# Splitting the first input tiles in two groups of four, with half a Q slice computed in between

## The chip, the cores and the metric

The kernel runs on one core of a Trainium2 chip. The metric is the device time of one execution in microseconds. The engines are PE (TensorE, matrix products), DVE (VectorE), ACT (ScalarE), POOL (GpSimd) and SP (SyncE, which here only issues transfers). They run side by side and wait for one another by semaphores.

## The reference

The input x has 4 batches of 1024 tokens with 1024 features. Two layers are computed:

```
x = x + attention(layernorm(x), Wq, bq, Wk, bk, Wv, bv)     # 16 heads of 64
x = x + layernorm(x) @ (ffn_weight * scale[:, None]).T + ffn_bias
layernorm(x) = (x - mean(x)) / sqrt(var(x) + 1e-5)          # no gain, no bias
```

The attention is local: a block of 128 queries sees 256 keys, 64 of them on either side of the block. 64 tokens of each head (the first, the last, and the 62 with the largest norm of q) see all 1024 keys instead. All is float32; the kernel gets that precision from PE by splitting each operand in a high and a low part (x = hi + lo) and summing three products, hi\*hi, hi\*lo and lo\*hi.

## The kernel before, in words

**Tiles.** A batch is 8 input tiles of 128 tokens by 1024 features (TILES = 8). The normalised batch stands transposed and split in xT_hi and xT_lo. The weights come in 24 slices of 128 output columns for each batch: 8 of Q, then 8 pairs of V and K. A slice is projected in two halves of 512 tokens (PSUM banks proj[0] and proj[1]). A half is 24 products of 128x128 by 128x512: 8 of w_hi with xT_hi, 8 of w_lo with xT_hi, 8 of w_hi with xT_lo (`project`, L439). `project_half` can issue them in two parts of 12.

**The order of the work** is written out by hand, one program for each engine. Every engine has an outer loop over the 4 batches (on PE at L628), and inside it loops over pairs of Q slices and over head pairs. In each batch PE projects the Q slices (`project_q`), then alternates attention of a head pair with the projections of the next (`attend`). Beside the last head pair of a batch (`ahead` is False) the tiles of the next batch are turned and split, so that the first projection of the next batch follows at once.

**The beginning of the program** has no attention to hide behind. For its 8 tiles:
- SP (L213 to L221) loads tiles 0 and 1, four small columns of constants (semaphore const_in, 64 when all are in), tiles 2 and 3, and each of tiles 4 to 7 when the tile four before it has landed; then two weight slices (L225) and the bias row.
- POOL (`split`, L324 and L326) makes w_hi and w_lo of weight slices 0 and 1 when they have landed.
- DVE waits for const_in, takes the moments of the tiles (`moments`, L895: two bn_stats a tile), and computes 1/sqrt of all 8 variances in one chain (`roots`, L908 to L918: 14 links, each waiting for the one before). Then it normalises each tile in place (`normalise`, L928) and subtracts for the low half (`rows_lo`, L960, two operations a tile), two tiles behind.
- PE turns each normalised tile by 8 transposes (`turn_rows`, L462), alternately into the banks of proj and of turn. Tile t waits for the low half of tile t - 2, which frees its bank.
- ACT casts the turned tile into xT_hi (`rows_hi`, L691, two operations a tile). The first activation of the program is preceded by the load of ACT's table.

When all 8 low halves are there (semaphores xT_set, waited for at the head of PE's outer loop), PE starts with slice 0.

Of the kernel before, what the change touches and what calls it, by code (L numbers as in the profile page):

```python
# [53 lines left out]
def build(nc, rows_in, wstream, bq, bk, bv, scale_ffn, bias_ffn, out):  # L54
# [7 lines left out]
    with ExitStack() as ctx:  # L62
# [134 lines left out]
        LAST_TILES = [[0], [1], [2], [3], [4], [5], [6], [7]]  # L197
        proj_banks, turn_banks = [proj[:, h, :] for h in range(2)], [turn[:, h * 512:h * 512 + 512] for h in range(2)]
# [231 lines left out]
        def _(pe):  # L430
# [195 lines left out]
            for t in range(TILES):  # L626
                turn_rows(q_store[:, t, :], t, (proj_banks, turn_banks)[t % 2], 2)
            with pe.Fori(0, BATCH) as n:  # L628
                for h in range(2):
                    pe.wait_ge(xT_set[h], (n + 1) * TILES)  # L630
                apart(pe)
                project_half(n, 0, 0, n * BUFS, 0)
                with pe.Fori(0, PAIRS // 4) as j:
                    project_q(n, j)
                project_q(n, PAIRS // 4, norms_too=True)
                with pe.Fori(PAIRS // 4 + 1, PAIRS // 2) as j:
                    project_q(n, j)
                project_half(n, PAIRS, 0, n * BUFS + PAIRS // 2, 1, (0,))
                turn_norms(n, 1)
                project_half(n, PAIRS, 0, n * BUFS + PAIRS // 2, 1, (1,))  # L640
                for half in range(2):
                    project_half(n, PAIRS + 1, 1, n * BUFS + PAIRS // 2, half)
                with pe.Fori(0, PAIRS - 1) as hp:
                    attend(n, hp, True)
                attend(n, PAIRS - 1, False)

# [34 lines left out]
        def _(act):  # L681
            for h in range(2):
                act.sem_inc(proj_free[h], 1)
            act.wait_ge(const_in, 64)
# [147 lines left out]
            for t in range(TILES):  # L832
                rows_hi(t, t, (proj_banks, turn_banks)[t % 2])
# [36 lines left out]
        def _(dve):  # L870
# [9 lines left out]
            dve.wait_ge(const_in, 64)  # L880
# [4 lines left out]
            def link_of(steps, links):  # L885
# [13 lines left out]
            def roots(steps, size=1, weight_scale=None):  # L899

                links = [1]
                link = link_of(steps, links)
                var, minus_half, bits, rstd, sq, less = (x[:, 0:size] for x in (ln_var, ln_minus_half, ln_bits, ln_rstd,
                                                                                ln_sq, ln_less))
                dve.wait_ge(ln_step, steps + 1)
                apart(dve)
                for i in range(size):
                    last = dve.bn_aggr(ln_mv[:, i, :], ln_stats[:, i, :, :].rearrange("p a b -> p (a b)"))  # L908
                link(last)
                dve.tensor_scalar(minus_half, ln_mv[:, 0:size, 1], EPS, -0.5, ALU.add, ALU.mult)  # L910
                link(dve.tensor_scalar(var, ln_mv[:, 0:size, 1], EPS, None, ALU.add))
# [19 lines left out]
            FIRST_STEPS = LN_LINKS  # L931
# [237 lines left out]
            for t in range(TILES):  # L1169
                dve.wait_ge(first_in[t % 4], 16 * (t // 4) + 16)  # L1170
                moments(q_store[:, t, :], t, last=(t == TILES - 1))
            roots(0, TILES)
            for t in range(TILES):
                normalise(q_store[:, t, :], q_store[:, t, :], t, xn_set)
                if t >= 2:
                    rows_lo(t - 2, t - 2, (proj_banks, turn_banks)[t % 2])
            for t in range(TILES - 2, TILES):
                rows_lo(t, t, (proj_banks, turn_banks)[t % 2])
# [104 lines left out]
```

## Time and profile before

| | |
|---|---|
| median of 3 runs | 2288.05 us (2286.37 to 2288.64) |
| the profiled execution | 2291.68 us, its span 2290.1 us |
| PE busy | 2194.3 us, 96% |
| DVE, ACT, POOL busy | 67%, 36%, 26% |
| granted clock of PE, mean | 0.989 of full speed |

The page's 40 slices cover 57 us each. Only in the first is PE poorly used (4 tenths). The granted clock reads 9 tenths or more in all slices but one. The chain that ended last runs over PE for 78% of the span and over DVE for 15%.

How to read it: busy time counts an engine as busy while an instruction of its is open. "issue" in the chain of waits is time in which an engine waited for nothing that the profile shows. An instruction can be open, and so count as busy, while it is waiting for something that no semaphore shows.

### The profile page before, as it was taken

The numbers are of one execution on the slowest core, as the hardware profiler recorded it, in microseconds if no ns is written. First come the engines' busy times: TensorE is split into PE (matmuls) and PEld (weight loads), VectorE is DVE, ScalarE is ACT, GpSimd is POOL, SyncE is SP. The second block draws the span as 40 slices with busy tenths as digits, with TensorE's granted clock in tenths as the row PEclk, the third lists the DMA queues.
The fourth block names the chain that finished last, engine by engine and source line by source line (L and its number), as shares of the span: only waits on it lengthen the run. The fifth ranks groups of instructions, "written<-read, shape, count | busy, mean of one in ns | idle before, by whom it ended". The sixth has DMA issues, their size and how long they took to land.

```text
span 2290.1 us, 41027 instructions
## 1 busy us (share of the span) xinstructions
PE 2194.3 (96%) x13024; PEld 1863.8 (81%) x13024; DVE 1536.3 (67%) x3450; ACT 835.2 (36%) x2201; POOL 601.6 (26%) x468
## 2 busy tenths in 40 slices
PE   4999999989999999899999998999999988999999
PEld 3878888868788888787888887878888876888887
DVE  5587776653877765738777657297776676666664
ACT  2224444443254454532444445224544450000000
POOL 1232232223232231232322312324123123222211
PEclk9999999999999999999999999999999998999999
DMA  3321111112211111123111110231111113333331
GB/s 120 87 89 43 51 58 43 49 34 79 89 48 53 58 41 50 32 78 92 49 51 53 46 53 31 65 97 58 39 51 60 40 33 139 126 135 137 137 129 73
DMA packets 106440, 160.04 MB, mean 70 GB/s; under 512 B 9648, under 2 KB 75254, under 8 KB 106352
## 3 DMA queue, kind: packets, MB, share of 16 engines
q1 hardware_dynamic: 98416, 140.03, 18.7%
q10 hardware_dynamic: 4608, 16.78, 1.8%
q0 software_dynamic: 3328, 2.17, 0.5%
q8 instruction: 42, 0.69, 0.1%
q14 instruction: 46, 0.38, 0.1%
HBM read 107.53 MB, written 51.41 MB: 69 GB/s over the span
## 4 chain that ended last, share of the span: by engine, by line
PE 78%; DVE 15%; issue 4%; ACT 2%; DVEq 0%; DMA 0%; SPq 0%; ACTq 0%
PE proj L439 36%; PE proj L661 15%; PE pv L532 8%; PE turn L522 5%; PE score L507 4%; PE pv L577 3%; PE score L558 2%; DVE x_norm L1003 2%; DVE top_idx L1001 2%; DVE top_val L999 2%; PE misc L545 1%; PE turn L652 1%; DVE q_sq L966 1%; DVE norms L968 1%; PE turn L568 1%
## 5 line engine op out<-in xcount | busy, mean ns | idle before, releaser
L439 PE MATMUL proj<-xT_hi,w_hi 128*128 128x512 f32 x1536 | 404.3, 405 | 11.8 <-issue 8.4
L439 PE MATMUL proj<-xT_hi,w_lo 128*128 128x512 f32 x1536 | 406.5, 398 | 0.0
L439 PE MATMUL proj<-xT_lo,w_hi 128*128 128x512 f32 x1536 | 381.0, 390 | 0.0
L439 PEld LDWEIGHTS proj<-xT_lo,w_hi 128*128 128x128 f32 x1536 | 288.3, 188 | 61.7
L439 PEld LDWEIGHTS proj<-xT_hi,w_lo 128*128 128x128 f32 x1536 | 283.9, 189 | 63.2
L439 PEld LDWEIGHTS proj<-xT_hi,w_hi 128*128 128x128 f32 x1536 | 276.9, 190 | 68.7 <-issue 11.3
L757 ACT ACTIVATE probs<-score,neg_max 128x256 f32<-128x256 f32 (+1 forms) x512 | 229.1, 460 | 165.2 <-DVE neg_max L1048 99.4
L334 POOL TENSOR_TENSOR ctx_out<-pv_sum,row_inv 128x256 f32<-128x256 f32 x128 | 87.9, 687 | 705.9 <-DVE pv_sum L1085 705.9
L326 POOL TENSOR_TENSOR w_lo<-w_raw,w_hi 128x1024 fp32r<-128x1024 f32 x98 | 243.4, 2483 | 7.9
L324 POOL CAST w_hi<-w_raw 128x1024 fp32r<-128x1024 f32 x98 | 106.1, 1083 | 501.7 <-PE proj L439 313.0
L532 PE MATMUL pv<-v_nat,pT_lo 128*128 128x128 f32 x1024 | 198.3, 275 | 0.0
L532 PE MATMUL pv<-v_nat,pT_hi 128*128 128x128 f32 x1024 | 194.3, 271 | 3.1 <-DVE pT_lo L1064 2.8
L1085 DVE TENSOR_TENSOR pv_sum<-pv,pv_lo 128x256 f32<-128x256 f32 x128 | 54.2, 424 | 185.5 <-ACT pv_lo L781 185.5
L966 DVE TENSOR_TENSOR q_sq<-q_nat 128x512 f32<-128x512 f32 x64 | 63.1, 986 | 168.4 <-ACT q_nat L707 167.4
L532 PEld LDWEIGHTS pv<-v_nat,pT_hi 128*128 128x128 f32 x1024 | 161.6, 191 | 15.5 <-issue 5.6
L1064 DVE TENSOR_TENSOR pT_lo<-turn,pT_hi 128x512 fp32r<-128x512 f32 x256 | 164.7, 684 | 11.5 <-ACT pT_hi L770 9.1
L532 PEld LDWEIGHTS pv<-v_nat,pT_lo 128*128 128x128 f32 x1024 | 155.4, 192 | 0.0
L419 POOL TENSOR_TENSOR q_store<-q_store,bias_b 128x1024 f32<-128x1024 f32 x32 | 76.6, 2396 | 286.4 <-DVE q_store L1232 284.9
L770 ACT CAST pT_hi<-turn 128x512 fp32r<-128x512 f32 x256 | 138.8, 597 | 7.7 <-PE turn L522 2.0
L522 PE MATMUL turn<-ident,probs 128*128 128x128 f32 (+1 forms) x1024 | 138.2, 277 | 3.5 <-ACT probs L757 3.5
L698 ACT ACTIVATE qT_cur<-proj,bq_c 128x512 f32<-128x512 f32 x64 | 44.1, 689 | 234.0 <-PE proj L439 234.0
L522 PEld LDWEIGHTS turn<-ident,probs 128*128 128x128 f32 (+1 forms) x1024 | 112.8, 138 | 6.6 <-ACT probs L757 6.5
(139 smaller groups left out, 3596.3 us busy)
## 6 DMA issues: line engine op xcount, KB each, us to landing
w_raw<-in_wstream SPq DMA_DIRECT2D x98, 512.0 KB, 3.8
q_store<-in_rows SPq DMA_DIRECT2D x36, 512.0 KB, 3.4
x_buf<-in_rows SPq DMA_DIRECT2D x36, 512.0 KB, 3.3
q_rows<-q_nat SPq DMA_DIRECT2D x64, 256.0 KB, 2.3
ctx_rows<-ctx_out SPq DMA_DIRECT2D x128, 128.0 KB, 1.8
q_store<-ctx_rows SPq DMA_DIRECT2D x32, 512.0 KB, 4.1
out<-q_store ACTq DMA_DIRECT2D x32, 512.0 KB, 2.6
bias_b<-in_bias_ffn SPq DMA_DIRECT2D x1, 512.0 KB, 7.6
```

The lines of the kernel that those rows point to most:

```text
L324: pool.tensor_copy(w_hi[b][:, :], w_raw[b][:, :]).then_inc(w_hi_set, 1)
L326: pool.tensor_tensor(w_lo[b][:, :], w_raw[b][:, :], w_hi[b][:, :].bitcast(F32), ALU.subtract).then_inc(w_split[b], 1)
L334: pool.tensor_tensor(ctx_out[:, s % 2].rearrange("p b h d -> p h b d"), pv_sum[:, s % 2].rearrange("p (h b) d -> p h b d", h=2), row_inv[: ...
L439: mm = pe.matmul(proj[:, half, :], w[b][:, k * P:k * P + P], x[:, k, half * HALF:half * HALF + HALF], start=(m == 0), stop=(m == 23), skip ...
L507: mm = pe.matmul(score[:, at:at + hi - lo], qs[r, i * BLK:i * BLK + BLK], ks[r, lo:hi], start=(first and b == 0), stop=stop, skip_group_ch ...
L522: mm = pe.transpose(turn[0:rows, col:col + P], probs[:, src:src + rows], ident[:, :])
L532: mm = pe.matmul(pv[:, g * P:g * P + P], pt[:, (g * 2 + c) * P:(g * 2 + c) * P + P], v_nat[:, 2 * s + b + c, h, :], start=(m == 0), stop=( ...
L661: mm = pe.matmul(proj[:, half, :], x[b][:, k * P:k * P + P], w[:, k, half * 512:half * 512 + 512], start=(m == 0), stop=(m == 23), skip_gr ...
L757: last = act.activation(probs[:, at:at + hi - lo], score[:, at:at + hi - lo], ACT.Exp, bias=neg_max[:, g:g + 1], accum_out=row_sum[:, g:g ...
L770: act.copy(pT_hi[:, h * 512:h * 512 + 512], turn[:, h * 512:h * 512 + 512]).then_inc(pT_hi_set, 1)
L966: dve.tensor_tensor(q_sq[:, :], src, src, ALU.mult).then_inc(q_squared[h], 1)
L1064: dve.tensor_tensor(pT_lo[:, cols], turn[:, cols], pT_hi[:, cols].bitcast(F32), ALU.subtract).then_inc(pT_set, 1)
```

## The change

Engine by engine:
- **DVE.** It no longer waits for const_in ahead of the first moments (it does so behind the last low half). Three operations on one column (q_sq from zero_c) are added at the top, of the kinds tensor_scalar with add and mult, tensor_scalar with a shift, and tensor_tensor with mult. `roots` can now work on four of the eight columns (`at`) and call a function between two links (`between`). The chain is run twice, for tiles 0 to 3 with the moments of tiles 4 to 6 between its links, and for tiles 4 to 7 with the low halves of tiles 0 to 2 between them.
- **ACT.** Instead of the wait for const_in there is a copy of one column of the identity at the top. The wait for const_in stands ahead of the last tile.
- **PE.** The turned tiles go to the banks of score and turn, so that proj is free. When tiles 0 to 3 are split the first part (12 products) of slice 0, half 0 is issued behind tile 4, the second part behind tile 5. The outer loop runs over 3 batches; each ends with the first half slice of the next, and the last batch stands as a copy behind the loop.

```diff
+        score_banks = [score[:, h * 512:h * 512 + 512] for h in range(2)]
+        FIRST = TILES // 2
...
-            for t in range(TILES):
-                turn_rows(q_store[:, t, :], t, (proj_banks, turn_banks)[t % 2], 2)
-            with pe.Fori(0, BATCH) as n:
+            def first_turn(t):
+                turn_rows(q_store[:, t, :], t, (score_banks, turn_banks)[t % 2], 2)
+
+            def first_q(n, tiles, part):
+                if part == 0:
+                    for h in range(2):
+                        pe.wait_ge(xT_set[h], tiles)
+                    apart(pe)
+                project_half(n, 0, 0, n * BUFS, 0, (part,))
+
+            def batch(n):
                 for h in range(2):
                     pe.wait_ge(xT_set[h], (n + 1) * TILES)
                 apart(pe)
-                project_half(n, 0, 0, n * BUFS, 0)
...
+            for t in range(FIRST):
+                first_turn(t)
+            first_turn(FIRST)
+            first_q(0, FIRST, 0)
+            first_turn(FIRST + 1)
+            first_q(0, FIRST, 1)
+            for t in range(FIRST + 2, TILES):
+                first_turn(t)
+            with pe.Fori(0, BATCH - 1) as n:
+                batch(n)
+                for part in range(2):
+                    first_q(n + 1, (n + 2) * TILES, part)
+            batch(BATCH - 1)
...
-            act.wait_ge(const_in, 64)
+            act.wait_ge(ident_set, 1)
+            act.copy(probs[:, 0:1], ident[:, 0:1])
...
-            dve.wait_ge(const_in, 64)
+            dve.wait_ge(edge_zero, 1)
+            dve.tensor_scalar(q_sq[:, 0:1], zero_c[:, :], EPS, -0.5, ALU.add, ALU.mult)
+            dve.tensor_scalar(q_sq[:, 1:2].bitcast(U32), zero_c[:, :].bitcast(U32), 1, None, ALU.logical_shift_right)
+            dve.tensor_tensor(q_sq[:, 2:3], zero_c[:, :], zero_c[:, :], ALU.mult)
...
             def link(ins):
                     links[0] += 1
                     ins.then_inc(ln_step, 1)
+                    if between is not None:
+                        between(links[0])
                     dve.wait_ge(ln_step, steps + links[0])
...
+            def late_moments(k):
+                if k % 3 == 0 and k < 3 * FIRST:
+                    first_moments(FIRST + k // 3 - 1)
+            def early_lo(k):
+                if k % 3 == 0 and k < 3 * FIRST:
+                    first_lo(k // 3 - 1)
+            for t in range(FIRST):
+                first_moments(t)
+            roots(0, FIRST, between=late_moments)
+            dve.wait_ge(first_in[3], 32)
+            moments(q_store[:, TILES - 1, :], TILES - 1)
+            for t in range(FIRST):
+                first_normalise(t)
+            roots(LN_LINKS, FIRST, at=FIRST, between=early_lo)
+            first_normalise(FIRST)
+            first_lo(FIRST - 1)
+            for t in range(FIRST + 1, TILES):
+                first_normalise(t)
+                first_lo(t - 1)
+            first_lo(TILES - 1)
+            dve.wait_ge(const_in, 64)
```

How this moves the instructions. First PE at the beginning of the program, before (L462 turns a tile, L439 are the products of a projection):

```order
L462 MATMUL turn<-ident,q_store 128x128 x8
L462 MATMUL proj<-ident,q_store 128x128 x8
L462 MATMUL turn<-ident,q_store 128x128 x8
L628 UNCONDITIONAL_BRANCH
L628 ISA
L447 ISA
```

and now, from tile 3 on (L464 turns a tile, L441 is a projection):

```order
L464 MATMUL turn<-ident,q_store 128x128 x8
L464 MATMUL score<-ident,q_store 128x128 x8
L441 MATMUL proj<-xT_hi,w_hi 128x512 x8
L441 MATMUL proj<-xT_hi,w_lo 128x512 x4
L464 MATMUL turn<-ident,q_store 128x128 x8
L441 MATMUL proj<-xT_hi,w_lo 128x512 x4
L441 MATMUL proj<-xT_lo,w_hi 128x512 x8
L464 MATMUL score<-ident,q_store 128x128 x8
L464 MATMUL turn<-ident,q_store 128x128 x8
L664 UNCONDITIONAL_BRANCH
```

The 24 products of slice 0, half 0 stand among the turns of tiles 5 to 7 and no longer behind them.

On DVE, the moments and the first links of the chain, before (L895 are moments, L908 to L916 the chain):

```order
L895 BN_STATS ln_stats<-q_store 128x6 x16
L908 BN_AGGR ln_mv<-ln_stats 128x2 x8
L910 TENSOR_SCALAR ln_minus_half<-ln_mv 128x8
L911 TENSOR_SCALAR ln_var<-ln_mv 128x8
L912 TENSOR_SCALAR ln_bits<-ln_var 128x8
L913 TENSOR_SCALAR ln_rstd<-ln_bits 128x8
L916 TENSOR_TENSOR ln_sq<-ln_rstd 128x8
```

and now (L926 are moments, L939 to L947 the chain, on four columns):

```order
L926 BN_STATS ln_stats<-q_store 128x6 x8
L939 BN_AGGR ln_mv<-ln_stats 128x2 x4
L941 TENSOR_SCALAR ln_minus_half<-ln_mv 128x4
L942 TENSOR_SCALAR ln_var<-ln_mv 128x4
L926 BN_STATS ln_stats<-q_store 128x6 x2
L943 TENSOR_SCALAR ln_bits<-ln_var 128x4
L944 TENSOR_SCALAR ln_rstd<-ln_bits 128x4
L947 TENSOR_TENSOR ln_sq<-ln_rstd 128x4
L926 BN_STATS ln_stats<-q_store 128x6 x2
```

The moments of tiles 4 to 6 come between the links of the first chain.

On PE at the end of a batch, before (L577 is the last product of the attention, L628 the outer loop, L652 the second layer, behind it):

```order
L462 MATMUL proj<-ident,q_store 128x128 x8
L577 MATMUL pv<-v_nat,pT_hi 128x256 x9
L577 MATMUL pv<-v_nat,pT_lo 128x256 x9
L628 REGISTER_ALU
L628 COMPARE_AND_BRANCH
L652 MATMUL turn<-ident,x_norm 128x128 x8
```

and now (L579 is the last product of the attention, L664 the outer loop, L642 the first inner loop of the next batch or of the copy):

```order
L579 MATMUL pv<-v_nat,pT_lo 128x256 x9
L634 ISA
L449 ISA
L450 ISA
L441 MATMUL proj<-xT_hi,w_hi 128x512 x8
L441 MATMUL proj<-xT_hi,w_lo 128x512 x8
L441 MATMUL proj<-xT_lo,w_hi 128x512 x8
L664 REGISTER_ALU
L664 COMPARE_AND_BRANCH
L642 UNCONDITIONAL_BRANCH
```

Before, the branch of the outer loop (L628) stood directly behind the last product of pv, and the half slice was the first thing behind its target.

## Rows read from the trace of the kernel before

**Rows 1.** Chain of waits, 0 to 60 us: start us, us, what.
```profile
6.79 9.60 DVE ln_stats L895 x16
...
24.65 0.82 DVE q_store L928
...
26.89 1.28 ACT L691
...
30.09 0.72 DVE q_store L928
...
34.65 1.20 DVE xT_lo L960 x2
...
42.41 12.83 PE proj L439 x48
...
55.68 5.49 PE proj L439 x24
```

**Rows 2.** Timeline of PE, the second half slice of the program.
```profile
49.64 1.98 PE L439 MATMUL proj<-xT_hi,w_hi 128*128 128x512 f32 x8
```

**Rows 3.** Stretch 43.8 to 47.2: us, PE busy, granted clock, DMA share, GB/s.
```profile
43.80:47.20 3.40, 3.40 (x10) 0.50 0.02 5
```

**Rows 4.** Chain of waits at the three batch boundaries.
```profile
499.13 1.23 PE proj L462 x8
500.35 2.15 PE pv L577 x18
502.50 3.60 issue
506.11 13.69 PE proj L439 x48
...
965.17 3.54 PE pv L577 x18
...
969.29 11.19 PE proj L439 x48
...
1427.61 4.24 issue
1431.85 13.33 PE proj L439 x48
```

**Rows 5.** Branches of PE's outer loop: the first, then all four (ns min/median/max).
```profile
L628 PEldq COMPARE_BRANCH  x1: 5292/5292/5292, 500.3 to 500.3; - x1
...
L628 PEldq COMPARE_BRANCH  x4: 67/4472/5921, 500.3 to 1890.3; - x4
```

**Rows 6.** Timeline of DVE: start us, us, engine, line, operation, out<-in.
```profile
17.27 2.32 DVE L910 TENSOR_SCALAR ln_minus_half<-ln_mv 128x8 f32<-128x8 f32 x1
...
20.83 2.18 DVE L916 TENSOR_TENSOR ln_sq<-ln_rstd 128x8 f32<-128x8 f32 x1
23.05 0.17 DVE L917 TENSOR_TENSOR ln_less<-ln_sq,ln_minus_half 128x8 f32<-128x8 f32 x1
23.25 0.17 DVE L918 SCALAR_TENSOR_TENSOR ln_rstd<-ln_less,ln_rstd 128x8 f32<-128x8 f32 x1
```

**Rows 7.** Timeline of POOL in the same stretch.
```profile
16.10 1.04 POOL L324 CAST w_hi<-w_raw 128x1024 fp32r<-128x1024 f32 x1 [13.73 <-DMA w_raw<-in_wstream]
17.23 2.34 POOL L326 TENSOR_TENSOR w_lo<-w_raw,w_hi 128x1024 fp32r<-128x1024 f32 x1
...
20.64 2.35 POOL L326 TENSOR_TENSOR w_lo<-w_raw,w_hi 128x1024 fp32r<-128x1024 f32 x1
```

**Rows 8.** Timeline of POOL and of DVE at 1908 us.
```profile
1908.04 4.73 POOL L419 TENSOR_TENSOR q_store<-q_store,bias_b 128x1024 f32<-128x1024 f32 x2 [1.50 <-DMA ctx_rows<-g_ctx,idx_cols]
...
1910.46 2.33 DVE L917 TENSOR_TENSOR ln_less<-ln_sq,ln_minus_half 128x1 f32<-128x1 f32 x1
```

**Rows 9.** Tile 3: its issue (timeline), its transfer (DMA view, last number us to landing).
```profile
4.54 0.43 SPq L218 DMA_DIRECT2D q_store<-in_rows  x1
...
q_store<-in_rows SPq DMA_DIRECT2D x1, 512.0 KB, 5.0
```

More of the change, by code:

```diff
@@ L832, in _ @@
             for t in range(TILES):
-                rows_hi(t, t, (proj_banks, turn_banks)[t % 2])
+                if t == TILES - 1:
+                    act.wait_ge(const_in, 64)
+                rows_hi(t, t, (score_banks, turn_banks)[t % 2])
             with act.Fori(0, BATCH) as n:
@@ L883, in _, with link_of @@
             turn8 = turn[:, :].rearrange("p (k t) -> p k t", k=KC)
-            def link_of(steps, links):
+            def link_of(steps, links, between=None):
                 def link(ins):
@@ L897, in moments, with roots @@
                     stats.then_inc(ln_step, 1)
-            def roots(steps, size=1, weight_scale=None):
+            def roots(steps, size=1, weight_scale=None, at=0, between=None):
                 links = [1]
-                link = link_of(steps, links)
-                var, minus_half, bits, rstd, sq, less = (x[:, 0:size] for x in (ln_var, ln_minus_half, ln_bits, ln_rstd,
-                                                                                ln_sq, ln_less))
+                link = link_of(steps, links, between)
+                var, minus_half, bits, rstd, sq, less = (x[:, at:at + size] for x in (ln_var, ln_minus_half, ln_bits, ln_rstd,
+                                                                                      ln_sq, ln_less))
                 dve.wait_ge(ln_step, steps + 1)
                 apart(dve)
-                for i in range(size):
+                for i in range(at, at + size):
                     last = dve.bn_aggr(ln_mv[:, i, :], ln_stats[:, i, :, :].rearrange("p a b -> p (a b)"))
                 link(last)
-                dve.tensor_scalar(minus_half, ln_mv[:, 0:size, 1], EPS, -0.5, ALU.add, ALU.mult)
-                link(dve.tensor_scalar(var, ln_mv[:, 0:size, 1], EPS, None, ALU.add))
+                dve.tensor_scalar(minus_half, ln_mv[:, at:at + size, 1], EPS, -0.5, ALU.add, ALU.mult)
+                link(dve.tensor_scalar(var, ln_mv[:, at:at + size, 1], EPS, None, ALU.add))
                 link(dve.tensor_scalar(bits, var.bitcast(U32), 1, None, ALU.logical_shift_right))
@@ L928, in normalise @@
                 dve.tensor_scalar(dst, src, ln_mv[:, i, 0:1], ln_rstd[:, i:i + 1], ALU.subtract, ALU.mult).then_inc(done, 1)
-            FIRST_STEPS = LN_LINKS
+            FIRST_STEPS = 2 * LN_LINKS
             ROW_STEPS = BATCH * TILES * (LN_LINKS + 2)
@@ L1167, in attend, with first_moments, first_normalise, first_lo @@
                 g_out(n, u, hp)
-            for t in range(TILES):
+            def first_moments(t):
                 dve.wait_ge(first_in[t % 4], 16 * (t // 4) + 16)
-                moments(q_store[:, t, :], t, last=(t == TILES - 1))
-            roots(0, TILES)
-            for t in range(TILES):
+                moments(q_store[:, t, :], t, last=(t == FIRST - 1))
+            def first_normalise(t):
                 normalise(q_store[:, t, :], q_store[:, t, :], t, xn_set)
[L1175 to L1178, printed above, removed]
+            def first_lo(t):
+                rows_lo(t, t, (score_banks, turn_banks)[t % 2])
+            def late_moments(k):
[19 more added lines that the diff above has]
+            dve.wait_ge(const_in, 64)
             with dve.Fori(0, BATCH) as n:
```

## The prediction

> **What bounds the kernel now.** I read the page first: PE is busy in 96% of the span, and in the 40 slices only the first one is poor (PE at 4 tenths). So a change to the beginning can win at most what PE lacks before its first projection. The chain of waits over the first 60 us says what that is [rows 1]: DVE takes the moments of eight tiles in one piece (6.79 to 16.39), a chain of small operations follows until 24.65, then tiles are normalised and split, and PE begins the first projection at 42.41. From there two half slices take 12.83 us, the second of them starting at 49.64 [rows 1, 2]. A half slice at the full clock takes 5.49 us, so the first one of the program, 7.23 us, paid 1.7 us for the lower level of the clock: 0.50 granted in 43.8 to 47.2 [rows 3].
>
> Second, the chain at the three places where one batch ends and the next begins. The diff moves instructions there too, though its title speaks of the beginning only. There PE stands for 3.60 us, 0.58 us (969.29 less the end of pv, 965.17 + 3.54) and 4.24 us, with nothing to wait for that the profile shows [rows 4], and the instruction that fills it is the branch at the end of PE's outer loop, which takes 5.29, 3.65 and 5.92 us (the row of all four gives 0.07, 4.47 and 5.92 as smallest, median and largest; the median is the mean of 5.29 and 3.65) [rows 5].
>
> **The small operations at 16.5 to 24.65.** The timeline of DVE shows some of them slow: 2.32 and 2.18 us, where such an operation takes 0.17 later [rows 6]. The change adds three tiny operations of the same kinds ahead of the first tile, as if these were costs of a first use. The timeline of POOL says something else [rows 7]: both end when a POOL instruction ends: 17.27 + 2.32 = 19.59 beside 17.23 + 2.34 = 19.57, and 20.83 + 2.18 = 23.01 beside 20.64 + 2.35 = 22.99. Late in the program, where these operations have run hundreds of times, it happens again: one takes from 1910.46 to 1912.79, beside two POOL operations that end at 1912.77 [rows 8]. So DVE's small operations on SBUF wait for POOL, and one link of the chain gets through at each gap between POOL instructions. The Trainium skill (GPSIMD Engine Reference, Specifications) has this as a shared SBUF interface, with "contention with DVE instructions in a 2-port perf mode or with two SBUF inputs". By that rule the three added operations buy nothing; the trace agrees (2.18 us for eight elements per row).
>
> **The new order of the beginning, step by step.** Times are of the profiled execution.
> - Tile 3 lands at 4.54 + 5.0 = 9.5 [rows 9]. The wait for the four constant columns (over at 6.79) no longer stands ahead of the moments, so those of tiles 0 to 2 are done before 9.5, and those of tile 3 at 10.7 (1.20 a tile, from 9.60 for eight).
> - Four aggregations and two operations: 0.7 us, to 11.5. Then moments of tile 4 (to 12.7), three links of 0.20, tile 5 (13.2 to 14.4), three links, tile 6 (14.9 to 16.1). Those of tiles 5 to 7 run later than in the kernel before, and of tile 4 within 0.1 us, so their data are there.
> - Five links are left at 16.1, and POOL's four operations for the first two weight slices hold 16.10 to 22.99. The gaps lie at 17.2, 19.6 and 20.6. As read above, two links pass at 17.2 (POOL waits for a semaphore there) and one at 19.6, and two at 20.6: the chain ends at 20.8, not at 17.1. The moments of tile 7 are not held (to 22.0). The first normalisation is held until 22.99 and ends about 23.5. Before it ended at 25.47. Of a possible 6 us the change gets 2.
> - Three more normalisations of 0.72 to 25.7. Meanwhile PE turns tile 0 and ACT casts it; the table load of 1.28 us [rows 1] is gone from this path since the added copy triggers it early. The second chain, with the low halves of tiles 0 to 2 between its links: 0.7 + 0.6 + 0.6 + 1.0 of its own and 3 x 1.20, to 32.0. Tile 4 normalised 32.8, low half of tile 3 34.0. Before that stood at 35.85 [rows 1].
> - Now PE alternates. First part (12 products, 12 x 0.229 = 2.75) from 34.4 to 37.1; turns of tile 5, 1.2 [rows 4], to 38.3; second part to 41.1; tile 6 to 42.3; tile 7 to 43.5. DVE waits twice for PE here: it has low half 5 at 39.6, 6 at 43.5 and 7 at 44.8. The second half slice can start at 45.1.
> - PE's clock: PE has some 2.6 us with nothing to do before tile 4 (30.5 to 33.1). Before, the clock read 0.50 behind a wait at the beginning [rows 3], and two half slices took 13.69 instead of 11 us after PE had stood for 3.60 [rows 4]. I take one stretch at 0.50, of which 1.4 us fall on this path: 46.5. It could cost nothing (45.1), or fall in the second half slice as well (48.2).
> So the second half slice begins at 46.5 where it began at 49.64: 3.1 us won, between 1.4 and 4.5.
>
> **The batch boundaries.** From the start of the 18 products of pv to the end of both first half slices (48 products) the three boundaries take 519.80 - 500.35 = 19.4, 980.48 - 965.17 = 15.3 and, with the same 2.15 for pv, 1445.18 - 1425.46 = 19.7 us, together 54.4 [rows 4]. In the changed kernel the first half slice of the next batch stands in the loop's body ahead of the branch, and the last batch is a copy behind the loop, so the third boundary has no branch. The branch not taken costs 0.07 us [rows 5]. Without gap and at the full clock a boundary is 2.15 + 11.19 = 13.3 [rows 4].
> - Third boundary: 13.3.
> - First and second: the branch still takes 3.7 to 5.9, but half a slice is queued before it. At the first boundary it began at 500.3 [rows 5], when the 18 products of pv had only just begun: PE's sequencer gets at least 17 products ahead. Here the last 17 x 0.229 are 3.9 us. What shows is 0 to 2 us; I take 1.0.
> - The clock. Before, the lower of its two levels (1.2 GHz of 2.4) cost 13.69 - 11.19 = 2.5 at the first, 3.54 - 2.15 = 1.4 at the second (in pv) and 13.33 - 11.19 = 2.1 at the third [rows 4]. PE had stood idle ahead of it, and most of that is gone; I take 1.0 for each.
> Sum 13.3 x 3 + 2 + 3 = 45.0, so 9.4 won. The ends: 40.0 (14.4 won); or a branch that shows in full (5.3 twice) and the old clock cost, 40.0 + 10.6 + 6.0 = 56.6 (2.2 lost). I stay near the first since the sequencer's lead is a measured one.
>
> The Trainium skill (Runtime: NRT & Kernel Launch, Instruction fetch mechanics) says that a taken branch to code outside the fetched pages "forces a DMA fetch of the target page before execution can continue", and that running on through straight code costs next to nothing. The trace's 5.3 us agree with the first; nothing here shows a copied batch yet. By the first alone, with nothing queued to hide it, the boundaries would come out as in rival 2.
>
> What else moves costs nothing: DVE's and ACT's later order is unchanged, and DVE's long stretch in the Q phase starts from Q tiles that PE delivers, so it shifts with PE. The copy of the last batch lengthens PE's program; I cost it at nothing, with up to 5.9 us if it must be fetched like a branch's target (rival 4).
>
> **The sum.** 3.1 + 9.4 = 12.5; take 12. The profiled execution took 2291.68 us with a span of 2290.1; the median of the runs is 2288.05, so I expect 2276.
>
> **Rivals.**
> 1. *First use after all.* If the added operations do remove the slow ones and POOL holds nobody, the chain ends at 17.1, the first normalisation at 19.1 instead of 23.5, and everything behind comes 4.4 us earlier: 2271.5. Against it: [rows 7, 8].
> 2. *Branch only moved.* If the sequencer cannot run ahead while it waits for the splits, the branch shows in full at two boundaries and only the third is won: 13.3 + 5.3 + 0.5, 13.3 + 3.7 + 0.5 and 13.3 come to 49.9, with the lower clock twice to 54; 0.5 to 4.5 us won there, total 2281 to 2284. For it: semaphore waits stand ahead of the half slice, too.
> 3. *Nothing to measure.* The alternation of PE and DVE eats the start (48.2 or later) and the boundaries give 1 us: 2285 to 2290.
> 4. *Slower: code must be fetched everywhere.* Place: PE at all three boundaries. The branch shows in full behind the half slice, and entering the copy costs a fetch too, each followed by the lower clock: three times 13.3 + 5.3 + 0.5 + 2.1 come to 63.6, 9.2 lost, 3.1 won at the start: 2294. It decides if more than 4 us stand at the third boundary in spite of straight code. Against it: a branch that is not taken costs 0.07 us [rows 5].
>
> **Chances.** Forecast (2272 to 2281) 0.55; rival 1 0.10; rival 2 0.17; rival 3 0.11; rival 4 0.07. A measurement of this kernel tells about 0.2%, 4.6 us, from no change, that is 2283.5. Forecast, rival 1 and nearly all of rival 2 lie beyond: faster 0.81; within 0.12; slower 0.07. The likeliest case alone spans 2272 to 2281; the range of eight in ten 2269 to 2285.
>
> **What would show it.** Right: bn_stats begin near 4.7; small DVE operations of 0.9 to 2.2 us remain between 16 and 21; the first normalisation ends near 23.5; the second half slice starts at 45 to 48; no PE gap over 0.5 us at the third boundary and gaps under 2 us behind the first half slice at the other two. Wrong: all small operations at 0.17 us (rival 1), gaps of 4 us between half slices (rival 2), a gap on entering the last batch (rival 4).

## The result and the profile after

| | before | after |
|---|---|---|
| median of 6 runs each | 2286.32 us (2285.39 to 2288.64) | 2277.19 us (2276.69 to 2277.57) |
| the profiled execution, its span | 2291.68, 2290.1 us | 2277.11, 2275.5 us |

By the medians the kernel is 9.1 us faster, 0.4%. The ratio on record is 0.9949, with a 95% interval of 0.9934 to 0.9965 (8 to 15 us), which holds the 0.9960 of the medians: the change is clear of the noise, its size is known to some 3 us. The forecast was 2276, with 2269 to 2285 as its range. All medians, ranges and intervals below leave out three executions that ran far slower (one of b_start_only at 2470.69 us, one of g_table_late at 11344.36, one of the kernel before at 3111.78).

The order of reading is that of the forecast: first the chain over the beginning, then the boundaries. The chain of waits of the changed kernel, 17 to 60 us (start us, us, what):

```profile
17.24 1.29 DVE ln_stats L926 x2
18.53 0.06 DVE q_store L959
18.59 1.30 issue
19.89 5.02 DVE q_store L959 x3
...
30.93 0.82 DVE q_store L959
31.76 0.14 issue
31.90 1.94 PE score L464 x8
33.84 3.48 PE proj L441 x12
37.31 0.87 PE turn L464 x8
38.19 2.77 PE proj L441 x12
40.96 0.45 PE score L464 x4
...
43.93 0.61 DVE xT_lo L991
44.54 0.42 issue
44.96 7.32 PE proj L441 x24
52.27 0.44 PE turn L470 x4
```

The timeline of DVE in the same stretch, which answers to [rows 6], has one slow link (0.89) and then the held normalisations:

```profile
16.13 0.89 DVE L948 TENSOR_TENSOR ln_less<-ln_sq,ln_minus_half 128x4 f32<-128x4 f32 x1
17.05 0.16 DVE L949 SCALAR_TENSOR_TENSOR ln_rstd<-ln_less,ln_rstd 128x4 f32<-128x4 f32 x1
...
18.45 6.47 DVE L959 TENSOR_SCALAR q_store<-q_store,ln_mv,ln_rstd 128x1024 f32<-128x1024 f32 x4
```

Both first half slices are done at 52.27; before it was 42.41 + 12.83 = 55.24 [rows 1]. That is 3.0 us. Two things in the rows of the chain still cost time. Three normalisations take 5.02 us, 1.67 each instead of 0.72. And the second half slice takes 7.32 us where one at the full clock takes 5.48. The stretches of PE show the clock at the second (us, busy time of PE, PEld, DVE, ACT, POOL with counts, granted clock, DMA share, GB/s):

```profile
40.80:45.30 4.50, 2.25 (x19) 1.97 (x18) 2.48 (x4) 3.21 (x6) 0.00 (x0) 1.00 0.01 4
45.40:48.80 3.40, 3.40 (x10) 2.67 (x9) 0.00 (x0) 0.00 (x0) 0.00 (x0) 0.51 0.00 0
48.80:52.20 3.40, 3.40 (x16) 2.75 (x16) 0.00 (x0) 0.00 (x0) 0.00 (x0) 0.99 0.00 0
```

PE was busy for 2.25 of the 4.50 us ahead of the half slice, and then one stretch of it was granted 0.51, the lower of the two levels, 1.2 GHz: the same that [rows 3] show of before, moved by 1.6 us. That the stop of 2.25 us is what brought the lower level isn't shown: after_again below has the same stop and the full clock behind it.

The chain at the three boundaries, to be held against [rows 4]:

```profile
498.39 2.15 PE pv L579 x18
500.55 5.46 PE proj L441 x24
506.01 0.36 issue
506.37 5.73 PE proj L441 x24
...
957.15 3.57 PE pv L579 x18
960.72 5.46 PE proj L441 x24
966.18 0.40 issue
966.59 5.73 PE proj L441 x24
...
1417.68 3.65 PE pv L579 x18
1421.33 10.91 PE proj L441 x48
```

The stops of 3.60 and 4.24 us are gone. What is left of the branch is 0.36 and 0.40 us between the two half slices. The three boundaries take 13.71, 15.17 and 14.56 us, 43.4 together against 54.4. The second and third owe 1.4 and 1.5 us to the clock: their 18 products of pv take 3.57 and 3.65 us instead of 2.15, and their stretch reads 0.50 (columns as above):

```profile
956.80:960.20 3.40, 3.40 (x19) 3.40 (x18) 1.38 (x2) 0.86 (x2) 0.00 (x0) 0.50 0.41 157
1417.60:1421.00 3.40, 3.40 (x18) 3.40 (x17) 1.29 (x2) 0.69 (x2) 0.00 (x0) 0.50 0.37 139
```

The branch itself has not become free. It takes 3.88 us at both boundaries, but it begins at 501.9, 1.4 us into the half slice, and so runs beside queued products (ns min/median/max, first and last start):

```profile
L664 PEldq COMPARE_BRANCH  x3: 67/3877/3881, 501.9 to 1422.7; - x3
```

### The profile page after: what moved, and what is told of

Its sections match the earlier page's. It is cut to its first block, busy times and chain, and to the rows that moved or that the text cites. A ratio compares the mean times of both kernels' runs of the same rounds, so it can differ in the third digit from the quotient of the medians.

```text
span 2275.5 us, 41042 instructions
## 1 busy us (share of the span) xinstructions
PE 2192.1 (96%) x13024; PEld 1863.5 (82%) x13024; DVE 1536.0 (68%) x3466; ACT 834.3 (37%) x2202; POOL 600.8 (26%) x468
## 4 chain that ended last, share of the span: by engine, by line
PE 79%; DVE 15%; issue 4%; ACT 2%; DVEq 0%; DMA 0%; SPq 0%; ACTq 0%
PE proj L441 36%; PE proj L684 15%; PE pv L534 8%; PE turn L524 5%; PE score L509 4%; PE pv L579 3%; PE score L560 2%; DVE x_norm L1034 2%; DVE top_idx L1032 2%; DVE top_val L1030 2%; PE misc L547 1%; PE turn L675 1%; DVE q_sq L997 1%; DVE norms L999 1%; PE turn L570 1%
## 5 line engine op out<-in xcount | busy, mean ns | idle before, releaser
L441 PE MATMUL proj<-xT_hi,w_hi 128*128 128x512 f32 x1536 | 402.5, 404 | 4.0 <-DVE xT_lo L991 2.3
L441 PE MATMUL proj<-xT_hi,w_lo 128*128 128x512 f32 x1536 | 405.7, 397 | 0.0
L441 PE MATMUL proj<-xT_lo,w_hi 128*128 128x512 f32 x1536 | 381.8, 391 | 0.0
L441 PEld LDWEIGHTS proj<-xT_lo,w_hi 128*128 128x128 f32 x1536 | 288.8, 188 | 62.3
L441 PEld LDWEIGHTS proj<-xT_hi,w_lo 128*128 128x128 f32 x1536 | 282.5, 189 | 62.6
L441 PEld LDWEIGHTS proj<-xT_hi,w_hi 128*128 128x128 f32 x1536 | 275.9, 189 | 60.2 <-issue 4.1
```

What stands on the lines that cost most here:

```text
L441: mm = pe.matmul(proj[:, half, :], w[b][:, k * P:k * P + P], x[:, k, half * HALF:half * HALF + HALF], start=(m == 0), stop=(m == 23), skip ...
```

## The experiments

They ran in three groups: a, c, d and f; before_again, after_again, e and df; b, g, i and j. Each group has its own runs of the kernel before (medians 2287.8, 2284.48 and 2286.95 us), to which the ratio refers. These medians differ by 3.3 us, so medians of different groups are compared only to some 3 us. One table holds all. "q turned" is when PE first turns a Q slice, which is when both first half slices are done. "Boundaries" is the time from the start of pv to the turn of the first Q slice of the next batch, summed over the three. "Rest" is the span less these two. Those three columns are of the one profiled execution, "median" and "ratio" of all runs.

| kernel | median us | ratio, 95% | q turned | boundaries | rest |
|---|---|---|---|---|---|
| before | 2286.32 | | 55.09 | 54.7 | 2180.3 |
| before_again | one run, 2290.13 | | 54.74 | 53.9 | 2179.8 |
| after | 2277.19 | 0.9949 (0.9934 to 0.9965) | 52.11 | 43.8 | 2179.6 |
| after_again | 2277.31 | 0.9966 (0.9952 to 0.9979) | 51.71 | 42.9 | 2182.3 |
| a_loop_only | 2277.33 | 0.9955 (0.9941 to 0.9969) | 54.87 | 44.2 | 2178.8 |
| b_start_only | 2286.14 | 0.9995 (0.9983 to 1.0007) | 53.18 | 49.3 | 2180.5 |
| c_no_warm | 2276.30 | 0.9955 (0.9941 to 0.9968) | 51.91 | 42.6 | 2179.3 |
| d_late_split | 2273.82 | 0.9941 (0.9927 to 0.9954) | 50.20 | 41.7 | 2180.3 |
| e_unrolled | 2275.34 | 0.9955 (0.9942 to 0.9969) | 52.45 | 41.9 | 2181.3 |
| f_no_turns_between | 2273.09 | 0.9942 (0.9928 to 0.9955) | 50.38 | 41.2 | 2179.6 |
| df_both | 2273.67 | 0.9949 (0.9935 to 0.9962) | 48.95 | 42.7 | 2180.5 |
| g_table_late | 2277.51 | 0.9958 (0.9943 to 0.9972) | 53.09 | 44.9 | 2181.4 |
| i_both_late | 2272.52 | 0.9937 (0.9924 to 0.9951) | 47.16 | 42.7 | 2182.4 |
| j_all | 2271.95 | 0.9933 (0.9920 to 0.9947) | 49.03 | 40.9 | 2182.6 |

The rest moves by up to 3.8 us between profiled executions of kernels that do the same there; no difference smaller than that is read from a span.

**The boundaries alone (a_loop_only): the kernel before with PE's loop of the changed kernel.**

```diff
-            with pe.Fori(0, BATCH) as n:
+            def first_q(n):
                 for h in range(2):
                     pe.wait_ge(xT_set[h], (n + 1) * TILES)
                 apart(pe)
                 project_half(n, 0, 0, n * BUFS, 0)
+
+            def batch(n):
...
+            first_q(0)
+            with pe.Fori(0, BATCH - 1) as n:
+                batch(n)
+                first_q(n + 1)
+            batch(BATCH - 1)
```

> The kernel before with one part of the change alone: the outer loop of PE runs over three batches and each ends with the first half slice of the next, the last batch is a copy behind the loop. The beginning of the program is as before. Theory (start and boundaries add up; the profiles give 3.0 us at the start): the boundary part is worth what is left of the 9.1 us, about 6 us: 2280.3 us. The first two branches show in less than 1 us, the third boundary has none. Rival (the gain is all made at the beginning): 2286.3 us, as before.

2277.33 us, 10.5 below the kernel before in its group. The rival is out, and the theory's 6 us was too low: by the medians this half of the change alone gives as much as the whole, to the 3 us that they can tell. Its profile has the loop's gain (boundaries 44.2) and the old beginning (54.87).

**The beginning alone (b_start_only): the changed kernel with the old loop, and no products between the turns.**

```diff
                 apart(pe)
+                project_half(n, 0, 0, n * BUFS, 0)
                 with pe.Fori(0, PAIRS // 4) as j:
...
-            first_turn(FIRST)
-            first_q(0, FIRST, 0)
-            first_turn(FIRST + 1)
-            first_q(0, FIRST, 1)
-            for t in range(FIRST + 2, TILES):
+            for t in range(FIRST, TILES):
                 first_turn(t)
-            with pe.Fori(0, BATCH - 1) as n:
+            with pe.Fori(0, BATCH) as n:
                 batch(n)
-                for part in range(2):
-                    first_q(n + 1, (n + 2) * TILES, part)
-            batch(BATCH - 1)
```

> The changed kernel's beginning on DVE and ACT, with the kernel before's outer loop on PE: four trips, the first half slice behind the head of the loop, no products between the turns of tiles 5 to 7. Theory (the beginning's gain is real and adds to that of the boundaries): PE reaches the first turning of q some 4.5 us earlier than in the kernel before (50.5 instead of 55.1 us, as in the variant without products between turns), the three boundaries take 53.5 to 54.5 us from the start of pv to the end of 48 products as before, and the median is 4 to 5 us below the kernel before's, ratio 0.998. Rival (the start's gain is lost again later, which would explain that the loop alone gave as much as the whole change): the same profile to 50 us, but the median within 1.5 us of the kernel before.

2286.14 us, 0.8 below the kernel before in the same group, and the interval of the ratio allows 3.9 us faster to 1.6 slower. The theory's 4 to 5 is out. The profile says which step of it was wrong: q is turned at 53.18 and not at 50.5, a gain of 1.9. The first half slice begins at 42.16, since at the head of the old loop it waits for all eight low halves, where in the changed kernel it waits for four. So it wasn't a gain lost later; most of it was never there. The timelines go further: the last low half ends at 41.83 here and at 42.08 before, 0.25 us earlier, and the 48 products take 11.18 instead of 12.83, because the lower clock (0.50 from about 34 to 40 us) fell on the turns this time. Tiles in groups of four bring DVE's end hardly earlier (in f_no_turns_between it is at 41.22); what the new beginning gives PE is a half slice that needs four tiles and not eight. The boundaries of this execution, 49.3, were also a surprise. The same old branch took 3.31, 5.44 and 3.65 us here, and 5.12, 5.30 and 3.47 in before_again, whose row reads:

```profile
L628 PEldq COMPARE_BRANCH  x4: 78/4292/5297, 499.8 to 1888.8; - x4
```

A branch standing open thus takes anything from 3.3 to 5.9 us, three times in each execution. In two groups the runs fit: those of the kernel before lie 7.3 us apart in the second (nine runs) and 10.9 in the third (16), those of after_again 2.1. In the first they don't: the kernel before is spread over 3.4 us there, and e_unrolled and j_all, which have no branch at all, over 3.9 and 4.1. So the branch is one source of spread among others.

**No branch of the outer loop at all (e_unrolled): the four batches written out.**

```diff
-            with pe.Fori(0, BATCH - 1) as n:
+            for n in range(BATCH):
                 batch(n)
-                for part in range(2):
-                    first_q(n + 1, (n + 2) * TILES, part)
-            batch(BATCH - 1)
+                if n < BATCH - 1:
+                    for part in range(2):
+                        first_q(n + 1, (n + 2) * TILES, part)
```

> The changed kernel with the four batches of PE written out one behind the other, so that no branch of the outer loop is left. Theory (a branch shows only 0.4 us since half a slice is queued before it, and straight code costs nothing): 0.8 us less, 2276.4 us, within the noise of the timing; the two gaps of 0.4 us are gone in the profile. Rival (each copy must be fetched at a price): 3 us or more slower, 2280 us.

2275.34 us (2273.41 to 2277.32), 2.0 below after_again beside it (2276.38 to 2278.49), but the intervals of the two ratios overlap, so a gain isn't shown. The first boundary takes 13.14 us, with no stop. Running on into straight code costs nothing that shows: the forecast's rival 4 and this experiment's rival are out. The profile shows the stops at two boundaries gone (0.23 us at the first in after_again, 0.36 and 0.40 in the changed kernel's first profile).

**The three added operations (c_no_warm).**

```diff
-            dve.tensor_scalar(q_sq[:, 0:1], zero_c[:, :], EPS, -0.5, ALU.add, ALU.mult)
-            dve.tensor_scalar(q_sq[:, 1:2].bitcast(U32), zero_c[:, :].bitcast(U32), 1, None, ALU.logical_shift_right)
-            dve.tensor_tensor(q_sq[:, 2:3], zero_c[:, :], zero_c[:, :], ALU.mult)
```

> The changed kernel without the three added one-column operations at the top of DVE. Theory (slow small operations wait for POOL): 2277.2 us, no change, the same operation held at 16.1 us. Rival (first use costs): three operations of 0.9 to 2.3 us come back where these kinds are first used, at about 11 to 13 us, and the time is 3 to 5 us longer, 2280 to 2282 us.

2276.30 us: they buy nothing that can be measured. The timeline of DVE without them (start, us, line, operation) has two slow operations:

```profile
16.38 0.90 DVE L944 TENSOR_TENSOR ln_sq<-ln_rstd 128x4 f32<-128x4 f32 x1
17.31 0.16 DVE L945 TENSOR_TENSOR ln_less<-ln_sq,ln_minus_half 128x4 f32<-128x4 f32 x1
17.51 2.19 DVE L946 SCALAR_TENSOR_TENSOR ln_rstd<-ln_less,ln_rstd 128x4 f32<-128x4 f32 x1
```

With all three in place the changed kernel has a slow one of 0.89 at 16.13 and held normalisations instead (above), and g_table_late, which has them too, shows 0.94 and 2.20. So they neither prevent the slow ones nor decide which they are.

**POOL's second split out of the way (d_late_split).**

```diff
-            for b in range(2):
-                split(0, b, b, 0)
+            split(0, 0, 0, 0)
+            pool.wait_ge(xn_set, TILES)
+            split(0, 1, 1, 0)
```

> The changed kernel, but POOL splits the second weight slice only when all eight tiles are normalised (it is needed some 20 us later). Theory (POOL's cast and subtraction of that slice hold DVE's normalisations, four of which took 6.47 instead of 2.96 us): they end 2.7 us earlier, the low half of tile 3 about 2.3 us earlier, and the time falls by 2 us to 2275.2. Rival (nobody is held by POOL, or it is hidden behind PE's slow turns): 2277.2 us.

2273.82 us, better than the 2275.2 expected, and 2.5 below c_no_warm in the same group. The four normalisations behind the chain take 2.97 us together, where they took 6.47 in the changed kernel. But they end at 24.10, only 0.8 earlier, since here the chain itself was held: two slow links, of 0.89 and 2.20 us, stood beside the first split. Against c_no_warm, whose chain was held the same way, they end 1.7 us earlier (25.80), and q is turned 1.7 earlier.

**Both splits out of the way (i_both_late), and no products between turns.** As above, with `pool.wait_ge(xn_set, TILES // 2 + 1)` ahead of slice 0.

> The changed kernel without products between turns and with both first splits of POOL moved away from DVE's chain: slice 0 waits until five tiles are normalised, slice 1 until eight are. Theory (POOL's operations are what holds the small operations and the normalisations): no operation of the first chain is slow, the chain ends at 17.1 us, the first normalisation at 19.2, the fourth at 21.4, tile 4 is normalised at 28.2; the split of slice 0 (3.4 us) now holds one normalisation of tiles 5 to 7 for about a microsecond; PE turns q first at 47.5 to 48.5, median 2271 to 2272. Rival (the slow operations are a cost of their first use or belong to their place in the program): they stay slow with POOL idle beside them, first normalisation at 22 or later, median 2273.5 as with slice 1 late alone.

The timeline of DVE, where POOL has nothing until 27.72:

```profile
15.73 0.17 DVE L949 SCALAR_TENSOR_TENSOR ln_rstd<-ln_less,ln_rstd 128x4 f32<-128x4 f32 x1
15.93 0.16 DVE L947 TENSOR_TENSOR ln_sq<-ln_rstd 128x4 f32<-128x4 f32 x1
16.12 0.16 DVE L948 TENSOR_TENSOR ln_less<-ln_sq,ln_minus_half 128x4 f32<-128x4 f32 x1
16.32 0.16 DVE L949 SCALAR_TENSOR_TENSOR ln_rstd<-ln_less,ln_rstd 128x4 f32<-128x4 f32 x1
16.52 1.29 DVE L926 BATCH_NORM_STATS2 ln_stats<-q_store 128x6 f32<-128x512 f32 x2
```

No link is slow, and q is turned at 47.16. That settles what holds DVE: take POOL's work away, change nothing on DVE, and every slow operation is gone. When POOL begins its split at 27.72, it comes back: the normalisation that starts at 30.55 takes 1.66 us. The median is 2272.52 us (2271 to 2272 was expected, and q at 47.5 to 48.5), 5.0 below g_table_late in the same group, which does what the changed kernel does apart from ACT's copy; by the times q is turned 5.9 were due. This run has f's order on PE too, so the 5.0 is the worth of both edits.

**No products between the turns (f_no_turns_between).**

```diff
-            first_turn(FIRST)
-            first_q(0, FIRST, 0)
-            first_turn(FIRST + 1)
-            first_q(0, FIRST, 1)
-            for t in range(FIRST + 2, TILES):
+            for t in range(FIRST, TILES):
                 first_turn(t)
+            first_q(0, FIRST, 0)
+            first_q(0, FIRST, 1)
```

> The changed kernel, but PE turns all eight tiles first and then issues the 24 products of the first half slice in one piece. Theory (DVE waited 2.5 and 1.6 us for turns that stood behind products, and PE then stood idle for 2.25 us before the second half slice, so putting products between the turns gave nothing): DVE ends its last low half at 39.8 instead of 44.5 us, the half slice runs beside that, and the second half slice ends at 50 to 51.5 instead of 52.3: 2275.5 to 2277 us. Rival (the early half slice between the turns is what the start wins): the second half slice ends 3 to 5 us later, 2280 to 2282 us.

2273.09 us, 3.2 below c_no_warm in the same group and below the 2275.5 to 2277 that were expected; the rival is out. Its chain:

```profile
36.63 1.94 PE score L464 x8
38.57 1.07 PE turn L464 x8
39.65 10.90 PE proj L441 x48
50.55 0.44 PE turn L470 x4
```

and the same stretch as the 0.51 above (columns as there):

```profile
45.40:48.80 3.40, 3.40 (x17) 2.81 (x16) 0.00 (x0) 1.18 (x2) 0.00 (x0) 1.00 0.00 0
```

The second half slice begins at 44.94 here and at 44.96 in the changed kernel. The first half slice was brought forward by 6 us there (33.49 instead of 39.40), and nothing behind it came earlier: the turns of tiles 5 to 7, and DVE's low halves of them, moved back in exchange, so PE then stood 2.25 us for the last of these. Here the first half slice covers DVE's last low halves, there is no stop, and 48 products take 10.90.

Part of that is where the clock falls. Every profiled execution of the new beginning has a stretch of 3 us or more at the lower level before q is turned, but not the same one. In the changed kernel's first profile it is in the second half slice. In after_again, c_no_warm and d_late_split it is in the first part, whose 12 products take 4.50, 4.58 and 4.58 us instead of 2.77; their second half slices follow the same stop of 2.25 us at 46.14, 46.32 and 44.61 and run at the full clock. e_unrolled and g_table_late have it in both places (second half slices of 7.32 and 7.37 us). In f_no_turns_between it is ahead of all products, among the turns. The stretch 34.20 to 37.60 in after_again and then in this kernel (columns as above):

```profile
34.20:37.60 3.40, 3.40 (x9) 2.65 (x8) 1.73 (x3) 0.44 (x1) 0.00 (x0) 0.50 0.00 0
34.20:37.60 3.40, 3.10 (x15) 2.57 (x14) 3.24 (x6) 1.76 (x3) 0.00 (x0) 0.50 0.00 0
```

So q is turned at 51.71 in after_again and at 51.91 in c_no_warm, near the 52.11 of the first profile, and all of them stand behind the 50.38 of this order. How much of the difference is the order itself and how much the place of the clock, one profile of it doesn't tell.

**Both of the last (df_both): the edits of d and of f.**

> The changed kernel with both edits that were faster by themselves: POOL splits the second weight slice only when all tiles are normalised, and PE turns all tiles before the first half slice in one piece. Theory (the first is felt through DVE, the second through PE, and now DVE's last tiles set the start of the half slice): 1.5 to 2 us less than the better of the two, 2271.5 us. Rival (both take away the same wait): 2273 us.

2273.67 us: the rival's 2273 is met. The profile has q turned 1.4 us earlier than f and 1.3 earlier than d; the medians (and the ratios, 0.9949 beside 0.9942 and 0.9941, since f and d are of another group) show none of it, which is within what they can tell.

**ACT's table load (g_table_late): the changed kernel without ACT's wait and copy at the top.**

```diff
-            act.wait_ge(ident_set, 1)
-            act.copy(probs[:, 0:1], ident[:, 0:1])
```

> The changed kernel without ACT's wait and copy at the top, so that ACT's table load (1.28 us) comes ahead of the first cast again. The prediction had the load leave the path. By the profile after, the first cast starts at 21.35 us and its low half only at 25.8, because the normalisations of tiles 0 to 3 are held until 24.91: theory, the load fits in that slack, nothing on DVE moves, median 2277.2 as the changed kernel. Rival (the load is on the path through the casts, which free no bank but feed the low halves): everything from the low half of tile 0 on 1.3 us later, median 2278.5.

2277.51 us, as the theory had it, but its reason was wrong. ACT's timeline of this kernel:

```profile
1.14 1.28 ACT L713 ACT_TABLE_LOAD   x1 [1.14 <-PEq L1310]
24.85 0.59 ACT L713 CAST xT_hi<-score 128x512 fp32r<-128x512 f32 x1 [22.43 <-PE score L464]
```

The load is at 1.14 us without the copy too. Before, it stood at 26.89, behind the wait of its cast for the first turned tile. The copy is not what moved it. What else differs at ACT's top is the wait for const_in: the three executions that have it there load at 26.70 to 27.01 us, all others at 1.14. No run moved that wait alone, so that it is the cause is argued and not shown.

**Everything together (j_all): i_both_late with the batches written out and without the three operations.**

> The same as the one with both splits late, and also no branch of PE's outer loop at all (the four batches written out) and without the three added DVE operations. Theory: two boundaries lose their 0.3 to 0.4 us between the half slices and nothing is added on running into straight code, 1 us in all: median 2270 to 2271. Rival (PE pays for fetching code that it has not run before, four times the length): 2273 or more.

2271.95 us, between theory (2270 to 2271) and rival (2273 or more), and not told apart from i_both_late's 2272.52. The boundaries are the shortest of all (40.9). The beginning is 1.9 us later in this execution: 1.3 because tile 3's moments began at 10.32 instead of 8.99, and 0.6 in the first 48 products (11.69 instead of 11.12). Both kernels beat g_table_late, which stands for the changed kernel in this group: it took 2276.6 us at least, their slowest runs 2274.6 and 2274.3.

**Both kernels again.**

> The kernel before once more, for its profile. Theory (its first profiled execution was 4 us over the median because the branch of the outer loop and the clock behind it vary between executions): the three boundaries take other times than 19.5, 15.4 and 19.8 us, in all 2 to 5 us less, and everything else agrees within 0.5 us. Rival (it varies elsewhere): the boundaries take the same again.

> The changed kernel once more, beside the others of this group. All theories: 2277 us. Its profile shows whether the small chain of DVE ends near 17.2 us (before POOL's first subtraction) or near 19.7 us (behind it): the profiled executions with the same order so far showed both, and I expect the first projection to start within 1 us of the same place either way.

The profiled executions of the kernel before (2291.68, 2290.13) both lie above every timed run of their groups (at most 2288.64 and 2288.83); those of after are within 1.2 us of their median. before_again's boundaries take 18.49, 18.60 and 16.85 us: each another time than in the first profile, as its theory had it, but in all only 0.8 less and not 2 to 5. after_again did as expected: its first projection starts at 33.67, beside 33.49.

## Why the prediction was right, and where its steps were off

**The start, 3.1 forecast, 3.0 measured, by steps that were off in both directions.** That the two numbers meet is partly luck: the steps below cancel.
- *Which operations POOL holds.* The mechanism was right (i_both_late), its victim was not. The forecast had two links through at 17.2, one at 19.6 and two at 20.6, the chain ending at 20.8 and the first normalisation at 23.5. In the changed kernel the held link of 16.13 came free at 17.02 and was the last but one, so the chain ended at 17.2; the moments of tile 7 followed, and the normalisations were held instead. PE turned tile 0 at 20.23. The holding was then paid in the three others (5.02 instead of 2.2 us). The four ended at 24.91 where 25.7 was forecast. In c_no_warm the chain was held much as forecast, and PE turned tile 0 at 23.89. It goes either way: of the nine profiles with this chain and POOL's first split beside it, after, after_again and f_no_turns_between have the chain through at 17.2 to 17.6, the six others have it held to 19.5 or later. The two ways differ by 3.7 us at tile 0, and by 1.4 when the second half slice begins (46.32 in c_no_warm), of which 1.1 is the first part at the lower clock (4.58 instead of 3.48).
- *POOL pays too.* POOL was slowed as well: its second pair took 1.50 and 2.69 us beside the normalisations, and 1.04 and 2.35 before [rows 7]:

```profile
19.37 1.50 POOL L326 CAST w_hi<-w_raw 128x1024 fp32r<-128x1024 f32 x1
20.95 2.69 POOL L328 TENSOR_TENSOR w_lo<-w_raw,w_hi 128x1024 fp32r<-128x1024 f32 x1
```

  The bn_stats of tile 7 ran at full speed beside POOL (1.29 us), and so did the low halves in i_both_late, which read PSUM. The Trainium skill (GPSIMD Engine Reference, Specifications) names DVE instructions in a 2-port mode or with two SBUF inputs; the trace agrees as far as both kinds were held here, normalisations with one SBUF input and products of two columns.
- *The alternation.* Low half 3 ended at 32.86 (34.0 forecast), the second half slice began at 44.96 (45.1 before the clock). 1.1 us of head start shrank to 0.1 in the alternation of PE and DVE.
- *The clock.* One stretch at the lower level was forecast, but at 1.4 us ahead of the second half slice. In the first profile it came inside it and cost 7.32 - 5.48 = 1.8; in after_again, c_no_warm and d_late_split it came ahead of it, as forecast, and cost 4.50 - 2.77 = 1.7 or 1.8; e_unrolled and g_table_late paid in both places.
- *The missed alternative.* The forecast priced the alternation as it stood and didn't ask what it bought. f_no_turns_between shows: no gain, and in the profiles q turned 1.3 to 1.7 us later (51.71 and 52.11 against 50.38).

**The boundaries, 9.4 forecast, 11.0 in the profile.** "Half a slice is queued before the branch" held: 0.36 and 0.40 us show, where 1.0 each was taken and 0 to 2 allowed. The third boundary has no stop, so rivals 2 and 4 are out. The clock cost 0, 1.4 and 1.5 us, where 1.0 each was taken. It now falls in pv, ahead of everything that the change touches, and with no such gap as the 3.60 us that the forecast made answer for it.

The Trainium skill (Runtime: NRT & Kernel Launch, Instruction fetch mechanics) has a taken branch to code outside the fetched pages wait for a fetch, and the fetches of straight code mostly hidden. The runs agree on straight code (e_unrolled, 13.14 us for a boundary), and the branch still takes 3.3 to 3.9 us when hidden; that it is a fetch that fills this time no trace shows. What is decisive, that the branch costs 0.4 us or less behind queued products, comes from the rows.

**The sum.** 14.0 us by the terms of the two profiles, 14.6 by their spans; 12.5 forecast and 9.1 by the medians. The step that was off is the one that took the terms of one execution as those of the median. The first profiled one (branches of 5.29, 3.65 and 5.92) lay 5.4 us above the median of its six runs. That its open branches, each between 3.3 and 5.9 us, explain this fits b_start_only (49.3 us at the boundaries instead of 54.7) but isn't shown: before_again lay 5.6 us above its group's median with other branches and nearly the same sum. That 2276 came out near 2277.2 is partly luck: the forecast took 12 from the median where the profiles have 14 and the medians 9.1, and the start's share of it, 3.1, hardly shows in the medians, while the loop's is larger than the 9.4 forecast (10.5 in a_loop_only).

**What stays open.** By the profile the start is worth 3.0 us; by the medians it shows as 0.8 (b_start_only, whose own profile has 1.9) and as 1.0 (c_no_warm against a_loop_only in the same group, 3.0 due). Both are within the intervals of some 3 us either way, so the start's gain is seen in the profiles only. Larger gains of the start do show: f_no_turns_between is 4.2 below a_loop_only in the same group, with 4.5 due from the start alone, and 3.0 more from boundaries that didn't show. Why an open branch takes sometimes 3.3 and sometimes 5.9 us, and never over 3.9 in 18 cases where products are queued before it, no run here tells.

## What to carry to other kernels

A change named for one place may be paid at another: here the loop alone gave the measured gain, and it was found by reading the diff for every instruction that moves past a branch. Put work ahead of a loop's long branch, so that the branch runs beside it. And bringing PE's work forward among its waits is worth only what comes earlier at the end of the stretch: keep it in one piece behind the last wait if it can cover another engine's tail. Before two profiles are compared, look where the lower clock fell in each; here it moved by 10 us between executions and cost the products 1.7 us or nothing.

## What the runs showed of the hardware that was not expected

- One and the same taken branch of PE took 3.3 to 5.9 us in the open (nine cases), and 3.3 to 3.9 with products queued.
- Four DVE normalisations of 1024 columns take 2.97 us alone, and 6.47 beside POOL; POOL's cast takes 1.50 instead of 1.04 beside it, so both sides pay.
- ACT's table load of 1.28 us came at 1.14 us of the program in a kernel whose first activation waits until 24.85 us, and behind that wait in another (26.89).
